# Experts' outputs written to the tokens' rows by indirect DMA, expert by expert, in place of gathers behind the last expert

## What is computed

```python
logits = x_flat @ router                      # T=2048 tokens, 8 experts
topk_logits, sel = top_k(logits, 2)           # each token goes to two experts
cw = softmax(topk_logits)
C = 640                                       # slots of one expert
pos = running count of tokens ahead of this one in its expert; valid = pos < C
buf[expert, pos] = x_flat[token]              # dropped where pos >= C
h = silu(gate) * up;  out_buf = h @ w_down    # 256 -> 176 -> 256, expert by expert
y[token] = sum over k of cw[k] * valid * out_buf[sel[k], pos[k]]
out = x + layernorm(y + shared_mlp(x_flat))   # shared: 256 -> 704 -> 256 for all tokens
```

## Time and profile before

| | |
|---|---|
| median of three runs | 846.82 us (839.72 to 848.85) |
| the profiled execution's own time | 842.17 us |
| its span in the trace | 840.4 us |
| busy in the span | PE 760.9, PEld (PE's weight loads) 634.0, DVE 614.5, ACT 490.4, POOL 553.7 us |
| granted TensorE clock, mean | 0.958 of full speed |

### The profile page before, as it was taken

How to read it: one execution, slowest core, us unless ns; L and a number is a source line. 1 busy time by engine, 2 the same in 40 slices (tenths; PEclk the granted TensorE clock), 3 DMA queues, 4 the chain that set the end, 5 groups by cost and what they waited for, 6 DMA issues and landing times.

```text
span 840.4 us, 13976 instructions
## 1 busy us (share of the span) xinstructions
PE 760.9 (91%) x4344; PEld 634.0 (75%) x4344; DVE 614.5 (73%) x1561; ACT 490.4 (58%) x1155; POOL 553.7 (66%) x460
## 2 busy tenths in 40 slices
PE   3867999999999999999999999998992989999875
PEld 3755787888888888888888888887781888887543
DVE  6637999887988977888877889886731177774337
ACT  2638677777767767666776677675520355542332
POOL 1347878898788987788987888871065534325751
PEclk9969999999999999999999999999995999999965
DMA  9121224441221222212221212210421345522321
GB/s 305 50 88 58 69 83 151 136 136 64 64 76 62 66 70 63 72 64 64 77 64 64 76 63 64 72 43 26 128 82 72 110 144 186 186 76 94 100 88 51
DMA packets 47701, 75.74 MB, mean 90 GB/s; under 512 B 9680, under 2 KB 24592, under 8 KB 47632
## 3 DMA queue, kind: packets, MB, share of 16 engines
q1 hardware_dynamic: 43744, 65.46, 24.3%
q0 software_dynamic: 3072, 8.39, 3.1%
q10 hardware_dynamic: 816, 1.05, 0.4%
HBM read 57.71 MB, written 17.17 MB: 89 GB/s over the span
## 4 chain that ended last, share of the span: by engine, by line
PE 75%; DVE 9%; ACT 5%; issue 5%; another core or an unknown queue 3%; POOL 2%; DMA 1%; DVEq 0%; ACTq 0%; POOLq 0%
PE ps L377 19%; PE ps L869 17%; PE ps L837 14%; PE ps L885 11%; PE ps L855 8%; PE ps L980 5%; DVE xn L1116 1%; DVE hid_both L1468 1%; DMA x_sb<-in_x_dram 1%; DVE hid_hi L1458 1%; DVE hid L1463 1%; DVE hid L1455 1%; DVE s_hid L1396 1%; ACT y_sb L750 1%
## 5 line engine op out<-in xcount | busy, mean ns | idle before, releaser
L589 ACT ACTIVATE prob<-ps,neg_max 128x512 f32<-128x512 f32 (+3 forms) x256 | 132.6, 526 | 86.2 <-DVE neg_max L1184 86.2
L869 PE MATMUL ps<-pt,vp 128*128 128x512 f32 (+3 forms) x512 | 150.7, 437 | 4.6 <-issue 3.1
L869 PEld LDWEIGHTS ps<-pt,vp 128*128 128x128 f32 x512 | 83.2, 192 | 54.6 <-issue 19.1
L1569 POOL TENSOR_TENSOR q_lo<-q_sw,q_hi 128x512 fp32r<-128x512 f32 x64 | 85.9, 1342 | 47.9 <-ACT q_hi L611 47.9
L1184 DVE CUSTOM_DVE_ANT_0 ps<-ps,causal_row 128x512 f32<-128x512 f32 (+3 forms) x256 | 117.4, 520 | 0.0
L1579 POOL TENSOR_TENSOR o_lo<-o_t,o_hi 128x512 fp32r<-128x512 f32 x64 | 83.3, 1301 | 47.3 <-ACT o_hi L617 46.8
L837 PE MATMUL ps<-k_hi,q_hi 128*128 128x512 f32 (+3 forms) x256 | 91.0, 355 | 7.3 <-POOL q_lo L1569 5.0
L855 PE MATMUL ps<-id_f,prob 128*128 128x128 f32 x640 | 92.3, 275 | 2.4 <-ACT pt L598 2.4
L1203 DVE TENSOR_TENSOR k_lo<-kh_row,k_hi 128x512 fp32r<-128x512 f32 x64 | 83.4, 1303 | 8.1 <-ACT k_hi L605 8.1
L1560 POOL TENSOR_TENSOR q_sw<-q_sw,rope_sb 128x512 f32<-128x512 f32 x64 | 83.7, 1307 | 8.7 <-ACT q_sw L578 8.7
L1565 POOL TENSOR_TENSOR q_sw<-q_cos,q_sw 128x512 f32<-128x512 f32 x64 | 81.5, 1274 | 9.2
(11 more groups left out here) (199 smaller groups left out, 1962.5 us busy)
## 6 DMA issues: line engine op xcount, KB each, us to landing
kh_row<-kvh_rows SPq DMA_DIRECT2D x64, 256.0 KB, 3.2
inv_row<-inverse_sums SPq DMA_DIRECT2D x64, 256.0 KB, 3.1
slot_inputs<-zeros SPq DMA_DIRECT2D x8, 640.0 KB, 4.8
xg<-slot_inputs SPq DMA_DIRECT2D x8, 640.0 KB, 4.6
slot_outputs<-yo SPq DMA_DIRECT2D x8, 640.0 KB, 3.3
up_raw<-in_w_up_dram SPq DMA_DIRECT2D x8, 368.0 KB, 4.8
x_sb<-in_x_dram SPq DMA_DIRECT2D x4, 512.0 KB, 9.1
wo_raw<-in_wout_dram SPq DMA_DIRECT2D x4, 512.0 KB, 8.0
```

The costliest lines, as they stand in the source:

```text
L589: ins = act.activation(prob[:, i % 2, ROW_AT[nt]:ROW_AT[nt] + w], ps_s[bank][:, at:at + w], ACT.Exp, scale=-1.0, bias=neg_max[:, i % 2, nt ...
L869: ins = pe.matmul(ps_qo[:, mt * P:SEQ], vp[:, b * TPB + mt, :], pt[:, i % 2, cols], start=(mt == 0), stop=(mt == PT_BANKS[-1][-1]))
L1569: pool.tensor_tensor(q_lo[:, i % 2, :], q_sw[:], q_hi[:, i % 2, :].bitcast(F32), ALU.subtract) \
```

## The change

Each row of `slot_inputs` grows from 256 to 258 numbers: behind the token's 256 values travel the slot number of the token's first choice and the token's own number. DVE makes the table of token numbers once, in attention unit 15 (`numbers`, six instructions), and `find_slots` puts two columns into `xn2`. After each expert's slots are loaded, DVE works out from the two columns in which row of a new DRAM tensor `token_outputs` (2 x 2048 rows, first choices in one half, second choices in the other) each slot's output belongs (`rows_of_slots`, four small instructions); an empty slot gets a number out of bounds, and its row is not written. POOL then scatters the expert's five output tiles with five indirect DMAs (`scatter_rows`). `token_outputs` is cleared beforehand by SP in units 12 to 19. Behind the last expert SP reads the rows back with 16 plain DMAs of 256 KB, two tiles each, into ten buffers. `slot_outputs`, its stores, the 32 gathers and the two instructions for their row numbers go. `yo` is held twice, and ACT waits for `yo_free` in place of the store. SP's waits in the loop change too: slots are loaded after `rows_ready` (before: after PE had turned the expert's slots), down weights after `dn_ready` (before: behind the store of `yo`).

```diff
+    EW = E + 2
-    yg_dram = nc.dram_tensor("slot_outputs", [NE * CAP, E], F32).ap()
+    yt_dram = nc.dram_tensor("token_outputs", [2 * T, E], F32).ap()
...
+                if 12 <= i < 20:
+                    n = i - 12
+                    sp.dma_start(yt_dram.rearrange("(p s) e -> p s e", p=P)[:, n * 4:(n + 1) * 4, :],
+                                 zeros[:, 0:E].unsqueeze(1).to_broadcast([P, 4, E])).then_inc(rows_cleared, 16)
...
                     if not last:
-                        sp.wait_ge(xg_psum, 3 * e + 3)
+                        sp.wait_ge(rows_ready, e + 1)
                         load_slots(e + 2, r)
                         sp.wait_ge(up_ready, e + 1)
                         load_expert(e + 2, r)
-                    sp.wait_ge(yo_ready, 3 * e + 6)
-                    sp.dma_start(yg_dram[bass.ds(e * CAP, CAP), :].rearrange("(p s) e -> p s e", p=P), yo) \
-                        .then_inc(yo_stored, 16)
                     if not last:
+                        sp.wait_ge(dn_ready, e + 1)
                         load_down(e + 2, r)
...
+            sp.wait_ge(yo_stored, NE * 16 * ST)
+            for g in range(TILES):
+                t, k = g // 2 * 2, g % 2
+                if g >= GR:
+                    sp.wait_ge(got_used, 2 * (g - GR) + 2)
+                rows = yt_dram[k * T + t * P:k * T + (t + 2) * P, :]
+                sp.dma_start(got[:, g % GR, :, :], rows.rearrange("(t p) e -> p t e", p=P)).then_inc(got_in[g % GR], 16)
...
+            def rows_of_slots(e, r):
+                dve.wait_ge(xg_in[r], 8 * (e - r) + 16)
+                dve.wait_ge(yo_free, e + 1)
+                dve.tensor_tensor(is_first[:], xg[:, r, :, E], slot_no[:], ALU.is_equal).then_inc(row_steps, 1)
+                dve.wait_ge(row_steps, 2 * e + 1)
+                dve.tensor_scalar(slot_no[:], slot_no[:], float(CAP), None, ALU.add)
+                dve.scalar_tensor_tensor(row_of[:], is_first[:], -float(T), xg[:, r, :, E + 1], ALU.mult, ALU.add) \
+                    .then_inc(row_steps, 1)
+                dve.wait_ge(row_steps, 2 * e + 2)
+                dve.tensor_scalar(to_row[:, r, :], row_of[:], SKIP, None, ALU.add).then_inc(rows_ready, 1)
...
+            def scatter_rows(e, r):
+                if e:
+                    pool.wait_ge(yo_stored, 16 * ST * e)
+                    pool.sem_inc(yo_free, 1)
+                pool.wait_ge(rows_ready, e + 1)
+                for k, (t0, n) in enumerate(YO_BANKS):
+                    pool.wait_ge(yo_ready, 3 * e + 3 + k + 1)
+                    for t in range(t0, t0 + n):
+                        pool.indirect_dma_start(
+                            yt_dram[:, :], bass.IndirectOffsetOnAxis(ap=to_row[:, r, t:t + 1], axis=0), yo[:, r, t, :],
+                            None, bounds_check=2 * T - 1, oob_is_err=False).then_inc(yo_stored, 16)
...
-            for e in range(NE + 1):
-                if e < NE:
-                    split_up(e, e % 2, e < 2)
-                if e:
-                    rest_of_down(e - 1, (e - 1) % 2)
+            split_up(0, 0, True)
+            split_up(1, 1, True)
+            for e in range(NE):
+                rest_of_down(e, e % 2)
+                if 1 <= e < NE - 1:
+                    split_up(e + 1, (e + 1) % 2, False)
+                scatter_rows(e, e % 2)
```

More of the change, by code:

```diff
@@ L166, in decoder_layer @@
         w0_lo = place("w0_lo", PT_AT + 5 * KB, [EO, 3 * P], F32R)
-        xn2 = place("xn2", R1, [TILES, E])
-        GR = 20
-        got = place("got", R1, [GR, E])
+        xn2 = place("xn2", R1, [TILES, EW])
+        GR = 10
+        got = place("got", R1, [GR, 2, E])
+        yo = place("yo", R1, [2, ST, E])
         after = [R1 + 20 * KB]
@@ L201, in decoder_layer @@
         at += EO * 2 * PART[1] * 4
-        xg = place("xg", at, [2, ST, E])
-        assert at + 2 * ST * E * 4 <= R2 + 32 * KB
+        xg = place("xg", at, [2, ST, EW])
+        assert at + 2 * ST * EW * 4 <= R2 + 32 * KB
         at = R2 + 32 * KB
@@ L228, in decoder_layer @@
         causal_row = small("causal_row", [SEQ])
-        zeros = small("zeros", [E])
+        zeros = small("zeros", [EW])
         vcol = small("vcol", [TPB, B * H])
@@ L241, in decoder_layer @@
         iota_sb = small("iota_sb", [NE])
+        below, token_no, slot_no = small("below", [1]), small("token_no", [TILES]), small("slot_no", [ST])
+        token_steps, slot_steps = small("token_steps", [NE]), small("slot_steps", [ST])
+        is_first, row_of = (small(n, [ST]) for n in ("is_first", "row_of"))
+        to_row = small("to_row", [2, ST], U32)
         group_w = [TPB * (B - 1), TPB]
@@ L247, in decoder_layer @@
         cw, pos, keep = (small(n, [2, TILES]) for n in ("cw", "pos", "keep"))
-        at_in, at_out = (small(n, [2, TILES], U32) for n in ("at_in", "at_out"))
+        at_in = small("at_in", [2, TILES], U32)
         id_in, rope_in, consts_in, w0_in = sem("id_in"), sem("rope_in"), sem("consts_in"), sem("w0_in")
@@ L330, in wo_head @@
             return i + WO_FIRST if i + WO_FIRST < H else None
+        NUMBERS_STEP = 15
         def y_tile(b, t):
@@ L1278, in rest_of_turned, with numbers @@
                                       ALU.subtract).then_inc(xt2_lo, 1)
+            def numbers():
+                done(dve.tensor_reduce(below[:], before_b[:], AX.X, ALU.add))
+                dve.scalar_tensor_tensor(token_steps[:], iota_sb[:], float(P), below[:].to_broadcast([P, NE]),
+                                         ALU.mult, ALU.subtract)
+                done(dve.scalar_tensor_tensor(slot_steps[:], below[:].to_broadcast([P, ST]), -float(ST), iota_sb[:, 0:ST],
+                                              ALU.mult, ALU.add))
+                for t in range(0, TILES, NE):
+                    dve.tensor_scalar(token_no[:, t:t + NE], token_steps[:], float(t * P + T - 1) - SKIP, None, ALU.add)
+                done(dve.tensor_scalar(slot_no[:], slot_steps[:], -float(ST), None, ALU.add))
             def split_shared(n):
@@ L1318, in _ @@
                     rest_of_wq(wq_head(i - 1))
+                if i == NUMBERS_STEP:
+                    numbers()
                 if i and wo_head(i - 1) is not None:
@@ L1471, in expert_steps @@
                         expert_rest(e + 1)
+                        rows_of_slots(e + 1, 1 - r)
             dve.sem_inc(gu_free, 2)
@@ L1477, in _ @@
             expert_rest(0)
+            rows_of_slots(0, 0)
             with dve.Fori(0, NE // 2 - 1) as pair:
```

44 lines of the change are left out of this document (16 added, 28 removed).

## The result

The changed kernel took 847.56 us (median of 20 runs, 842.15 to 849.46). The kernel before took 843.31 us in 20 runs beside it (839.72 to 848.85). The ratio is 1.0038, 95% between 1.0023 and 1.0053. The forecast was 836 us. The range of 821 to 855 held the time, but the sign was wrong.

A forecast was written before the change was run, and what follows sets the result against it. The loop was taken as near PE's pace, the tail as stalled by the gathers, with POOL to pace the changed loop. 842.2 - 17.6 + 8.0 + 0.5 = 833.1, plus 3 for the median: 836 us, range 821 to 855.

The forecast's parts named there:

- the sign: Whole kernel: forecast faster, 836 us against the profiled execution's 842.2 and the three runs' median of 846.8.
- The tail: Behind the last expert: without gathers PE and DVE run free of stalls, 17.6 us less.
- rival 4: Stalls are not the gathers' doing, or return in the loop with the scatters; 851 us, chance 0.19.
- The reads: Plain reads on SP replacing the gathers: hidden, with next to nothing to spare for the first batch.
- The scatter's price: Five scatters per expert on POOL in the loop: pitch 1.36 us, from the common 1.28 plus 0.08 for busy DVE.
- Rival 3: Scatters in the loop slowed by a busy DVE to near 2.1 us, deciding from 1.67; 855.6 us, chance 0.15.
- The rule of the Trainium skill: GpSimd can't write descriptors during VectorE's two-port copy (620 ns become 3100), so conversions of hid_hi and hid2 would delay scatters.
- The free edits: Outside loop and tail: clearing, longer rows and `find_slots` cost nothing; `numbers` costs 0.5 us.
- the sum for the loop: Expert loop: POOL's low parts 4.45, scatters 6.4, gaps 0.4 make 11.25 us an expert; loop 8.0 us longer.
- the term for POOL's queue: Expert loop: low parts and scatters queued on POOL make it the slowest engine, loop 8.0 us longer.
- the prediction's criterion: Right if POOL is busy nearly all loop, PE waits for `dn_lo` or `w_lo`, and an expert takes 11.3 to 12 us.

The follow-up runs named there:

- b_split_late: Kernel before with only POOL's order of low parts changed to the changed kernel's (split of e+1 behind down weights of e): 861.03 us, ratio 1.0206.
- b_plain_reads: Kernel before with its 32 gathers replaced by 16 plain reads on SP, which sum wrong rows: 826.14 us, ratio 0.9806.
- b_gather_pause: Kernel before with POOL waiting after every eighth gather until it has landed, three waits: 829.38 us, ratio 0.9844.
- b_window4: Kernel before with POOL waiting ahead of each gather until the fourth gather before it has landed: 841.98 us, ratio 0.9996.
- b_pause16: Kernel before with a single pause of POOL, after the sixteenth gather until it has landed: 829.14 us, ratio 0.9844.
- a_no_scatter: Changed kernel with the 40 scatters of the experts' outputs left out, POOL's changed order kept: 843.81 us, ratio 1.0022 to before.
- a_split_ahead: Changed kernel, scatters kept, with POOL splitting expert e+2's up weights behind e's down weights, as before did: 835.18 us, ratio 0.9914 to before.
- a_split_wait: Changed kernel, own order, with POOL's split of e+1 waiting until DVE has finished e's hidden values: 837.21 us, ratio 0.9930 to before.

## Why the prediction was wrong

**The tail was right.** Forecast were 17.6 us less; measured are 17.7 (85.2 to 67.5). The steps hold one by one. The second cut is 22.9 us later than in before. With these taken off, the six sums of `shared_sum` on DVE start at 790.8, 791.7, 804.3, 805.2, 813.7 and 816.1; the prediction had 790.8, 791.6, 804.4, 805.1, 813.6 and 816.1. The last two are these, and the very last starts 6.65 us ahead of the end at 845.6, where the prediction took 6.7:

```profile
836.55 0.69 DVE L1432 TENSOR_TENSOR y_sb<-ps,y_sb 128x512 f32<-128x512 f32 x1
838.95 0.69 DVE L1432 TENSOR_TENSOR y_sb<-ps,y_sb 128x512 f32<-128x512 f32 x1
```

Neither has a wait, where the last in before waited 1.78 us for PE. The stalls were the gathers' doing, which the first half of rival 4 denied. Its second half, that scatters in the loop bring them back, is wrong too: series of five show no such gaps in PE's or DVE's rows.

**The reads were right.** SP issued them from 787.79 on, and DVE never waits for `got`:

```profile
795.67 3.37 DVE L1534 SCALAR_TENSOR_TENSOR y_sb<-got,cw,y_sb 128x256 f32<-128x256 f32 x8
```

**The scatter's price was right.** The profile's page gives 40 in 41.2 us, 1.03 us each, and 0.30 us stand between two in a row: 1.33 us of pitch where 1.36 was taken.

```profile
L1705 POOL DMA_INDIRECT token_outputs<-yo,to_row x40 | 41.2, 1030 | 34.3 <-ACT yo L745 24.3
```

Rival 3 fell with it. It needed 1.67 us. The longest in the loop took 1.23 us, and one behind it, at 779.34 beside DVE's `w_lo<-sw_raw,w_hi`, took 1.98. One in 40 took what the rival wanted for all. The rule of the Trainium skill that the prediction named beside this rival did not show at the hidden values either: the scatter at 743.03, with DVE's conversion into `hid_hi` starting at 743.57 within it, took 0.97 us as elsewhere. It was the conversion that got longer, 0.59 us in place of 0.33.

**The free edits were free, as far as can be told.** The routing window 600:673 is the same within a microsecond of PE. The loop begins 1.5 us later (679.3 against 677.8), where 0.5 was forecast. In five runs of kernels that are the same as before up to there (b_split_late, b_plain_reads, b_gather_pause, b_window4 and b_pause16) it begins anywhere from 678.5 to 681.0, so a cost of 1.5 us for clearing and `numbers` can't be told from none.

**The step that failed is the sum for the loop.** It said: "With 0.4 us of gaps this is 11.25 us, so POOL becomes the slowest engine of the loop by 0.7 us an expert". It counted POOL's instructions in a queue of their own, and compared that queue with the loop's pace of before, as if they couldn't change the durations of other engines. (Nor did it have a term for PE's clock in the loop, though the prediction had said of the tail that a stall costs twice.) The order shown with the change said that `split_up(e+1)` had moved to where `split_up(e+2)` stood, and that step was priced at nothing, without a reason. It should have been followed to its neighbour on DVE. Its real price is 18.4 us (a_no_scatter, b_split_late). It comes from 8.3 us more of `hid_lo`, which PE waits for and whose waits then lower its clock. With the old order the term for POOL's queue is right: 8.6 us against the 8.0 forecast (a_split_ahead), and 835.2 us against 836.

So the prediction's criterion, that POOL is busy nearly all through the loop and PE waits there for `dn_lo`, is nearly met in a_split_ahead (POOL busy 64.6 of 86.0 us, with 0.30 us between its scatters besides) and not in the kernel after. That kernel's POOL is busy for 65% of the loop, and PE waits for DVE.

**The contention was sought on the wrong side.** The Trainium skill (SBUF — State Buffer, "Who interferes with whom") was cited for VectorE holding up GpSimd's descriptors. The 620 and 3100 ns quoted with it stand further up on that page of the Trainium skill, in "A bandwidth-pool intuition that's wrong (but worth ruling out)". The same section of the Trainium skill, "Who interferes with whom", says that a VectorE instruction with two SBUF inputs contends with a GpSimd instruction that reads SBUF. It says that one with a single SBUF input doesn't, outside the two-port modes, and that the order of issue decides which of the two is held up. The trace agrees: `hid_lo` has both inputs in SBUF and took 1.96 us when it came 0.14 us behind POOL's `w_lo`; `xg_lo`, with one in PSUM, took 1.62 us for three with POOL's `w_lo` beside it and without; and the small `is_first`, with two, took 1.19 us where it takes 0.15 in the changed kernel, and ended as `w_lo` did. That section, held against the list of what moved, would have pointed at this step. The size of the loss comes from a_no_scatter and b_split_late.

**What the sum is made of.** Before's span is 840.4. The start is 1.5 us later, the loop 21.4 longer, the tail 17.7 shorter: 845.6, the span of the changed kernel. Of the 21.4 us, 18.4 are the order, and the scatters on top of it 3.0; with the order restored the scatters and what goes with them cost 8.6, since POOL is then the one that PE waits for most. While PE waits for DVE anyway, most of what POOL does is hidden.

## What to carry to other kernels

When an edit moves an instruction on one engine, ask beside which instruction of its partner it will now run, and not only how long its own queue gets. Beside the wrong one it can hold the other engine for nearly its own duration, and PE's clock can fall behind the wait. So an added wait that keeps the two apart can win time: here 1.1%. A long unbroken series of indirect DMAs can be broken by one wait of 2.6 us, which is worth trying before the data flow is rewritten.

## What was not expected of the hardware

**POOL holds DVE.** A 128x320 subtraction on DVE took 0.49 us alone and 1.96 us when POOL's 128x736 subtraction had started 0.14 us before it. Six of sixteen met it, which gives 1064 ns on the mean. With an operand in PSUM there was no such effect: three `xg_lo` took 1.62 us with POOL's `w_hi` and `w_lo` beside them and without.

**PE's clock is half of the price.** Behind each wait of 2.4 to 2.8 us for `hid_both` PE ran 3 us at a granted clock of 0.50 to 0.54. In a_split_wait no wait for POOL or DVE in the loop was longer than 2.1 us, and the granted clock stayed at 1.00.

**An unbroken series of indirect DMAs stalls other engines, after a while.** Series at a pitch of 1.28 to 1.31 us left PE and DVE alone for their first 14 us in the routing stage (from 612.6, the first scatter, to 626.7, where DVE stands) and for some 25 us in the tail. Then PE, its weight loads, DVE and ACT stand, most often with "issue" or "remote" as the only cause in the profile. Series of 8 and of 5 showed no such gap; of two series of 16 the second did, once, 19 us after its start (b_pause16). A pause until the last has landed ends the effect, and a limit of four under way, which didn't make POOL wait, does not. What fills up in that time, and why its onset differs between the two stages, stays open: nothing in the traces names a queue or a count for it, and no run here varied the pitch. Every execution timed here was also recorded by the profiler, so no run shows whether the stalls would be there without it.
